# Rounding the second bf16 part of q and k on ScalarE in a decoder layer's first close stage

## The reference

```python
x = layernorm(x + linear_attention(x))        # 16 heads, 128 random features
x = layernorm(x + softmax_attention(x, mem))  # 16 heads of 16, 154 memory keys
x = layernorm(x + mixture_of_experts(x))      # 16 experts, top 4, and 2 shared
```

```python
y = num / den                                 # per head
x = layernorm(x + y @ W_proj + b_proj)
q, k, v = split(x @ W_attn + b_attn)          # of the softmax attention
```

## Time and profile before

| what | value |
|---|---|
| median of 3 runs | 2217.79 us (2216.48 to 2221.77) |
| profiled execution | 2214.3 us; its span in the profile 2212.2 us |
| first close stage, from the first projection of q and k to the last copy of v | 585.2 to 720.4 us |
| busy over the span | PE 84%, DVE 67%, ACT 41%, POOL 18% |
| granted TensorE clock, mean of the span | 0.925 |

### The profile page before, as it was taken

The page is one execution under the profiler, slowest core; times in us unless marked ns, Lnnn a source line. Parts: engine busy times, 40 slices in busy tenths (PEclk is TensorE's granted clock), DMA queues, the critical chain, the costliest instruction groups (busy, mean ns, idle before and its releaser), DMA issues. The chain is left out here.

```text
span 2212.2 us, 38875 instructions
## 1 busy us (share of the span) xinstructions
PE 1867.3 (84%) x13696; PEld 1218.1 (55%) x13696; DVE 1486.7 (67%) x3864; ACT 912.7 (41%) x1398; POOL 389.1 (18%) x511
## 2 busy tenths in 40 slices
PE   7914999999688058989989999956689999999997
PEld 4603766767455013333333333324478888888886
DVE  7921554555598167888878888523498877777776
ACT  5602554555233005656656666721333233323322
POOL 2110212110332501111111111255220000000000
PEclk9966999999899558999999999978899999999999
DMA  6961554543388410221222120336500000000000
GB/s 171 222 136 62 121 104 109 111 108 111 116 224 203 113 64 18 74 71 59 73 73 63 62 84 32 110 114 206 162 23 29 30 1 30 29 14 17 20 10 10
DMA packets 167359, 187.39 MB, mean 85 GB/s; under 512 B 80816, under 2 KB 137536, under 8 KB 161044
## 3 DMA queue, kind: packets, MB, share of 16 engines
q1 hardware_dynamic: 131456, 136.45, 21.4%
q0 software_dynamic: 18976, 28.01, 6.7%
q10 hardware_dynamic: 16756, 20.56, 3.5%
HBM read 114.33 MB, written 70.20 MB: 83 GB/s over the span
## 5 line engine op out<-in xcount | busy, mean ns | idle before, releaser
L1402 ACT ACTIVATE sa_prob<-sa_ps_s 128x1024 f32<-128x1024 f32 (+3 forms) x480 | 376.3, 825 | 337.2 <-PE sa_ps_s L1310 194.0
L1460 DVE CUSTOM_DVE_ANT_0 sa_ps_m<-sa_ps_m,sa_later 128x282 f32<-128x282 f32 (+4 forms) x640 | 278.5, 461 | 102.7 <-PE sa_ps_m L1283 101.4
L1463 DVE TENSOR_REDUCE sa_piece_max<-sa_ps_m 128x1 f32<-128x512 f32 x384 | 259.2, 688 | 36.6 <-PE sa_ps_m L1283 36.1
L1283 PE MATMUL sa_ps_m<-sa_k,sa_q 96*128 96x358 bf16 (+7 forms) x1024 | 259.4, 304 | 8.7 <-DVE sa_piece_max L1460 6.9
L1801 DVE SCALAR_TENSOR_TENSOR mo_acc<-mo_ps_o,mo_keep,mo_acc 128x256 f32<-128x256 f32 x512 | 212.2, 477 | 71.5 <-PE mo_ps_o L216 71.3
L1438 POOL TENSOR_SCALAR_AFFINE_SELECT sa_prob<-sa_prob 128x256 f32<-128x256 f32 x256 | 102.5, 406 | 579.6 <-ACT sa_prob L1402 576.7
L686 DVE TENSOR_TENSOR la_att<-la_ps_att,la_cap 128x512 f32<-128x512 f32 x128 | 88.3, 690 | 171.6 <-PE la_ps_att L587 171.6
L1667 ACT ACTIVATE mo_h_hi<-mo_h 128x512 fp32r<-128x512 f32 x144 | 91.0, 632 | 272.6 <-DVE mo_h L1783 270.4
L1281 PEld LDWEIGHTS sa_ps_m<-sa_km,sa_q 96*128 96x128 bf16 x512 | 50.7, 99 | 240.6 <-issue 146.6
L1281 PE MATMUL sa_ps_m<-sa_km,sa_q 96*128 96x154 bf16 x512 | 122.9, 245 | 70.3 <-DMA sa_q<-s_q_parts 51.2
L1310 PE MATMUL sa_ps_s<-sa_q,sa_k 99*128 99x512 bf16 (+3 forms) x768 | 180.4, 331 | 2.1 <-ACT sa_prob L1402 2.0
(11 more groups left out here) (197 smaller groups left out, 3835.7 us busy)
## 6 DMA issues: line engine op xcount, KB each, us to landing
s_y<-la_y SPq DMA_DIRECT2D x16, 512.0 KB, 2.9
s_x<-cl_xn SPq DMA_DIRECT2D x16, 512.0 KB, 6.1
s_y<-sa_y SPq DMA_DIRECT2D x16, 512.0 KB, 2.7
mw_raw<-experts SPq DMA_DIRECT2D x18, 384.0 KB, 4.5
s_q_parts<-pj_parts SPq DMA_DIRECT2D x16, 384.0 KB, 5.2
s_k_parts<-pj_parts SPq DMA_DIRECT2D x16, 384.0 KB, 2.6
s_q_parts<-cl_parts SPq DMA_DIRECT2D x16, 384.0 KB, 7.8
s_k_parts<-cl_parts SPq DMA_DIRECT2D x16, 384.0 KB, 6.8
```

Source lines behind the costliest of these rows:

```text
L1283: last = nc.tensor.matmul(ps_m[:, s, a - lo:hi - lo], qs, k[g][0:STACK, j, a - MEM:hi - MEM], start=lo > 0, stop=True, skip_group_check=True)
L1402: nc.scalar.activation(dst, src, ACT.Exp, scale=HD ** -0.5).then_inc(expd[s], 1)
L1460: nc.vector.tensor_tensor_reduce(ps_m[:, s, 0:hi - lo], ps_m[:, s, 0:hi - lo], later[:, BANK + lo - first:BANK + hi - first], 1.0, -BIG, A ...
L1463: nc.vector.tensor_reduce(piece_max[:, j, t, n:n + 1], ps_m[:, s, 0:hi - lo], AX.X, ALU.max).then_inc(piece_done[s], 1)
```

## The change

The casts of line 1046 leave VectorE's program one for one: part 1 of each slice is rounded on ScalarE by a copy (function second), and VectorE's last subtraction of the slice waits for it. Per tile ScalarE gets four activations, two behind the evacuations of slice 1 and two behind those of slice 3. Each waits for VectorE's first subtraction of its slice (semaphore qk_rest), and VectorE's second subtraction waits for it (qk_second). VectorE's two chain links within a split are gone.

```diff
--- before.py
+++ after.py
@@ -749,6 +749,7 @@
             ps_qk = ph.ps("ps_qk", [P, 2, TILE])
             ps_v = ph.ps("ps_v", [P, TB, C])
             qk_ps, v_ps, qk_first = ph.sem("qk_ps"), ph.sem("v_ps"), ph.sem("qk_first")
+            qk_rest, qk_second = ph.sem("qk_rest"), ph.sem("qk_second")
             qk_full = ph.sems("qk_full", 2)
             qk_split = ph.sems("qk_split", 2)
             v_full = ph.sem("v_full")
@@ -993,6 +994,13 @@
                             act.wait_ge(qk_split[s % 2], n * (NS // 2) + START)
                             nc.scalar.activation(full[:, s], ps_qk[:, s % 2], ACT.Identity,
                                                  bias=bias_qk[:, s:s + 1]).then_inc(qk_full[s % 2], 1)
+                            if s % 2:
+                                second(n, s - 1)
+                                second(n, s)
+
+            def second(n, s):
+                act.wait_ge(qk_rest, n * NS + s + 1 + START)
+                nc.scalar.activation(parts[:, s, 1], rest[:, s], ACT.Copy).then_inc(qk_second, 1)
 
             row(0, True, True)
             with act.Fori(1, B - 1) as b:
@@ -1040,12 +1048,9 @@
                 for s in pair:
                     dve.wait_ge(qk_full[s % 2], use(b, half, s) + 1 + START)
                     dve.wait_ge(qk_first, tile(b, half) * NS + s + 1 + START)
-                    ins = nc.vector.tensor_tensor(rest[:, s], full[:, s], parts[:, s, 0], ALU.subtract)
-                chain.link(ins)
+                    nc.vector.tensor_tensor(rest[:, s], full[:, s], parts[:, s, 0], ALU.subtract).then_inc(qk_rest, 1)
                 for s in pair:
-                    ins = nc.vector.tensor_copy(parts[:, s, 1], rest[:, s])
-                chain.link(ins)
-                for s in pair:
+                    dve.wait_ge(qk_second, tile(b, half) * NS + s + 1 + START)
                     nc.vector.tensor_tensor(parts[:, s, 2], rest[:, s], parts[:, s, 1],
                                             ALU.subtract).then_inc(qk_split[s % 2], 1)
```

## The result

The changed kernel took 2230.4 us (median of 8 runs, 2222.55 to 2238.4), the kernel before on the same chip 2218.57 us (8 runs, 2215.32 to 2224.76). The ratio is 1.0053, 95% interval 1.0038 to 1.0068: 12 us slower. The forecast was 2215.8 us, range 2208.5 to 2223.5, with 0.63 on no change. Its time, its range and its sign are wrong.

A forecast was written before the change was run, and what follows sets the result against it. VectorE was taken as the close stage's tightest engine, busy 16.82 of 17.77 us a turn. Terms -0.6 -3.1 +4 x 0.25 +0.2 gave -2.5, taken as -2.0 us; forecast 2215.8 us, range 2208.5 to 2223.5.

The forecast's parts named there:

- Nothing outside the stage is touched: Whole kernel outside the first close stage: no change; the two new semaphores count as nothing, under 0.2 us at most.
- Part 1: Close stage, VectorE: with the casts gone, the subtractions of line 1049 inherit the stall beside GpSimd; the first casts took 4.96 us.
- only casts meet GpSimd: Rival, close stage: subtractions run free beside GpSimd; -11 to -16 us, 2202 to 2207; chance 4%.
- Part 2: Tile 0 of the close stage: start not moved, the first pair of last subtractions ends earlier; gain 0.6 us.
- Part 3: Second pair of casts, slices 2 and 3: moving them is worth nothing while TensorE's output projection covers it, else 0.5 us a turn.
- Part 4: ScalarE's queue: five loads and the evacuation wait behind the slice 3 cast; projection at M+6.15 instead of M+4.53, 1.6 us later.
- M: Moment when VectorE starts a tile's last pair of subtractions in the close stage; one turn M to M is 17.77 us.
- Part 5: Close stage loads land at M+13.6, 3.9 us behind need; first such turn gains 3.1 us, later turns take 18.0.
- the forecast's loop: Close stage turns after the first late-load turn: cast, loads, landing 12.1, line 850, subtractions, line 851; 18.0 us against 17.77.
- landing 15 us behind issue: Rival, close stage: late GpSimd meets no two-input operation in most turns; turns average 16.8 us, whole -6 to -8; chance 15%.
- Clock: TensorE idles in two places a turn; one low-clock stretch more or less is 1.7 us, widening each case and deciding none.
- Collision with the writes: Rival, close stage: late loads collide with k's writes; each us of landing beyond 12.1 costs one a turn; about +8, 2226; chance 18%.

The follow-up runs named there:

- 24 pads: Kernel before, plus 24 increments of an unused semaphore on ScalarE ahead of its softmax attention loop; 2239.28 us against 2221.36, ratio 1.0074.
- 32 pads: Kernel before, plus 32 increments of an unused semaphore on ScalarE ahead of its softmax attention loop; 2218.03 us against 2219.0, ratio 0.9993.
- 28 or 12: Kernel before, plus 28 or 12 unused semaphore increments on ScalarE ahead of its softmax loop, one run each; 2220.3 us with 28, 2219.19 us with 12.
- after_104_pads: Changed kernel, plus 104 unused semaphore increments on ScalarE ahead of its softmax loop; 2213.83 us, ratio 0.9966 to the kernel before.
- 6 pads: Changed kernel with ScalarE's loads issued ahead of the casts of slices 2 and 3, plus 6 unused increments ahead of its softmax loop; 2210.58 us, ratio 0.9959.
- first pair alone: Against the kernel before, only casts of slices 0 and 1 go to ScalarE; 16 unused increments ahead of its softmax loop; 2211.62 us, ratio 0.9969.
- 8 pads: Changed kernel, plus 8 unused semaphore increments on ScalarE ahead of its softmax loop; 2212.66 us, ratio 0.9956 to the kernel before.
- 20 pads: Kernel before, plus 20 unused semaphore increments on ScalarE ahead of its softmax loop, a single run; 2220.8 us.
- loads first: Changed kernel with ScalarE's loads issued ahead of the casts of slices 2 and 3, plus 104 unused increments ahead of its softmax loop; 2210.67 us, ratio 0.9943.

## Why the prediction was wrong

**The step that failed** is the sentence "Nothing outside the stage is touched", behind which two semaphores stood at under 0.2 us. ScalarE's program grew by 24 instructions ahead of the softmax attention, and its loop came to lie where ScalarE fetches instructions about twice as often. That costs 18 us: 0.81% between the kernel before with 24 and with 32 pads, three turn-backs of 3.6 to 10.9 us each. With about -8 for the stage that gives +10, measured is +12. The waits of the kernel before have no row on issue for ScalarE in the attention, so nothing in that profile showed the price; but the edit's 24 instructions could be counted, and that a program's length ahead of a later loop may matter was left out of the sum and of the rivals.

What the runs show of the mechanism: the loss comes and goes with the loop's place alone (24 pads, not 28 or 12). At the bad places ScalarE's queue fetches about twice as much inside the loop (10 to 12 packets from 1000 to 1200 against 5), and the long waits on issue end 1.6 to 2.2 us behind the start of such a packet. How much of it is waited for depends on the work that stands between the loop's start and the wait. The page "Runtime: NRT & Kernel Launch" of the Trainium skill (section "Instruction fetch mechanics") says that a taken branch whose target isn't in the two blocks held forces a fetch before execution goes on. The waits near the jump, and their going away with the place, agree; but the longer one stands behind the first exp and not at the jump itself, of which the page says nothing. The page gives blocks of 16 KiB with 256 instructions; the packets here are 8 KB (0.57 MB in 70). By its figures a packet would hold 128 instructions, an estimate; after_104_pads, 128 places on, is back at no wait, which agrees, though other shifts are good too. A loop of 266 instructions, ScalarE's as counted, touches three blocks of 128 at most places and four at nine of 128, and this fits all seven places tried. So does the page's own block of 256, of which the loop touches two at most places and three at nine of 256. The runs don't tell the two apart, and which blocks ScalarE keeps was not measured.

**Part 1, the stall is inherited: right.** 5.60 us for the first pair of line 1054 in tile 0, and as much for that of line 1062 where the loads were in time (5.60 in five of six turns with 6 pads). The rival in which only casts meet GpSimd is out.

**Part 2, tile 0: right in kind.** The prediction had 0.6 us, from the end of the pair. In tile 0 of the kernel after, the normalisation starts 11.16 us behind the projection (596.99 - 585.83), 0.8 earlier than the 11.95 of before; the turns with loads in time are shorter by as much (17.0 against 17.77).

**Part 3, the second pair is worth nothing: right,** shown by the first pair alone.

**Part 4, the loads queue behind the cast: right, its price too low.** The projection stands at M+7.15 in tile 1 and at M+6.40 with 8 pads (608.30 - 601.90), forecast 6.15; the first turn is 18.9 us with 8 pads (589.44 to 608.30), by the forecast's terms 17.77 - 0.6 + 1.6 = 18.8. From the first load's issue to the end of the last took 4.7 us in tile 1 (599.59 to 604.31), where 3.6 was counted. Five waits of TensorE for line 980 make 7.8 us in the kernel after.

**Part 5, mis-sized: the landing.** I took 12.1 us from the first load's issue to GpSimd's start. Of the kernel with 8 pads:

```profile
618.67 1.44 ACTq L194 DMA_DIRECT2D c_y<-s_y  x2
...
632.22 0.68 DVE L1051 TENSOR_TENSOR cl_rest<-cl_full,cl_parts 128x512 f32<-128x512 f32 x1
633.48 2.36 POOL L851 TENSOR_TENSOR cl_yn<-c_y,c_inv 128x1024 f32<-128x1024 f32 x1 [3.77 <-DMA c_x<-x]
...
636.31 3.44 DVE L1054 TENSOR_TENSOR cl_parts<-cl_rest,cl_parts 128x512 bf16<-128x512 f32 x2
```

It took 14.8 us there (618.67 to 633.48), and 13.8 to 14.7 in the other four turns. The turn behind tile 1 is still as forecast (next M after 14.8 us, forecast 14.6). But GpSimd now comes in later than line 1051, in part or wholly. Its stall falls on line 1054 of the last pair, behind which nothing is due, since the next projection waits for ScalarE's loads anyway. So the five turns behind the first average 16.7 us (608.30 to 691.97), where the forecast's loop had 18.0, and the stage takes 127.2 us, 8.0 less than before. The prediction had the very case as a rival at 0.15: landing 15 us behind issue, turns of 16.8, -6 to -8 us. It was the right one for the stage's turns.

**Clock.** Part of the 8.0 us goes with the clock. Two turns of the old stage, 19.5 and 19.6 us at a granted clock of 0.91, are 3.6 us longer together than two of 17.77; with 8 pads the clock is 1.00 in every turn of the stage. Against the old stage without such turns (133.0 us with 20 pads) the gain is 5.8 us. With loads first it is 0.8 us in each of six turns, 4.8 us, and the rest of its 8.7 is the same two turns. Whether the change keeps the clock up or the profiles fell so isn't shown: the first pair alone and the loads first with 6 pads have one such turn each. The prediction's rival on the clock gave 1.7 us to one stretch more or less, the right size. The kernel after itself (130.4 us, turns of 17.2) and the one with 104 pads (135.8) had stretches at a lower granted clock; 656 to 676 in the kernel after:

```profile
656.00:676.00 20.00, 17.68 (x55) 11.29 (x54) 13.75 (x26) 8.25 (x13) 6.12 (x3) 0.83 0.75 203
```

Here TensorE, which idled until 655.22 for line 980, was granted 0.83 on average and the turn took 20.8 us. With late loads the stage thus varies between 127 and 136 us from profile to profile; the old stage took 135.2 to 135.4 in six of its seven profiles and 133.0 in one. The medians at good places hold -6 to -8 us (0.9966 and 0.9956 against 0.9993).

**Collision with the writes: no loss, though the landing grew.** Line 991's wait for the writes of k is 0.7 us in the kernel after and 5.1 with 8 pads, against the 8.5 for both the earlier trace rows. The landing grew by 1.7 to 2.7 us over the 12.1 counted, and this rival priced each us of that at a us a turn. That price failed: the turns got shorter, since with GpSimd that late the stall falls where nothing waits for it.

**What stays open:** why the landing took 13.8 to 14.8 us and not 12; and the whole price of the third turn-back, which loses 10 us where the others lose 2 to 4. It has two waits on issue, 2.1 and 4.9 us, and in the kernel before no wait for TensorE stands there that could cover them: the first exp of the turn follows the last copy at once (1309.39 behind 1308.90), where at the first jump it waited 2.97 us. That leaves 3 us open. Open are also the 5.7 us behind the attention, which appear in kernels with the old stage too and don't show in their medians (0.9993 with 32 pads). The late loads themselves cost little or nothing: 0.9956 with 8 pads beside 0.9959 with the loads first at the same place.

## What to carry to other kernels

An edit that adds instructions to one engine's program moves every loop behind it. Before a loss or gain of under 1% is put down to the edit, compare each engine's waits on issue inside the later loops, and its packets on the instruction queue; if they changed, run the old kernel with as many empty instructions ahead of the loop. A stall between VectorE and GpSimd isn't removed by taking the stalled instruction away: it goes to the next one, and the gain is what no longer stands behind it (0.8 us a turn here, of 4.2 us seen). A wait for another engine holds back the loads that stand behind it in the same program; whether that costs depends on what the late data then collide with, and here the medians show no loss. Before a gain in a stage is put down to an edit, compare the granted clock of its turns: it made 3.6 of 8.0 us here.

## What was not expected of the hardware

- Eight empty instructions more ahead of ScalarE's loop take away 18 to 22 us: the changed kernel goes from 1.0053 to 0.9956 of the kernel before, and with the old stage 24 and 32 are at 1.0074 and 0.9993.
- At a loop's turn ScalarE stands idle for 4.9 to 5.8 us if one exp stands ahead of the fetch's boundary; with three it doesn't at two of the turn-backs, and for 3.5 us at the third. The third has a second wait, ahead of its first exp, of 2.0 to 2.1 us in all three kernels with a bad place.
- The five DMA issues of ScalarE hold back the evacuation behind them by 3.3 to 4.1 us though nothing else is waited for, five times in the stage of the kernel after:

```profile
ACT cl_xT L980 <- issue: 18.3, 5, 4.1
```
